# A decoder layer with routed experts on one core: routing of the first tiles inside the loop, routing lots and the prologue laid out anew

## The chip, the core and the metric

The kernel runs on one core of a Trainium2 chip. The core has five engines with a queue each: TensorE (PE, with its weight loads shown as PEld) multiplies matrices into eight PSUM banks, VectorE (DVE), ScalarE (ACT) and GpSimd (POOL) work on SBUF and PSUM, and SyncE (SP) issues most of the DMAs. An engine runs its queue in order and waits on semaphores that other engines or DMAs raise. The metric is device time in microseconds, lower is better.

## What is computed

Eight tiles of 128 rows with 256 features go through self attention, cross attention and a feed-forward part with 16 routed experts and a shared one:

```python
x = x + attn(layernorm(x), Wq, bq, Wk, bk, Wv, bv, Wo, bo)       # 16 heads, 4 key groups, rope, sliding mask
x = x + xattn(layernorm(x), ctx, ctx)                            # 16 heads, causal, keys = values = ctx
h = layernorm(x)
shared = silu_and_mul(h @ shared_gate_up_w.T) @ shared_down_w.T * sigmoid(h @ sgate_w.T)
w = softmax(h @ gate_w.T); top_w, top_ids = top_k(w, 4)
for e in range(16):
    coef = sum(where(top_ids == e, top_w, 0))
    acc += (silu_and_mul(h @ w13[e].T) @ w2[e].T) * coef
x = x + shared + acc
```

## The kernel before

Each engine's queue is written out by hand; no scheduler orders anything. A tile is one batch entry.

**Prologue.** GpSimd clears constants; TensorE runs bf16 matmuls on zeros (`keep_clock`, counts in `WARM`) between the first real steps. For tile f, `front_n` (VectorE) writes the first norm, `front_a` turns it on TensorE, `front_b` projects it to `qkv`, `front_r` (VectorE, L865) adds the bias, `turn` (GpSimd, L481 to L485) applies the rotation, `front_p` (VectorE, L870) pads the keys, and `front_c` turns queries and keys into the layout of the scores. `first_norms` makes the statistics of the input tiles, in lots of 2, 2 and 4 tiles.

**The loop.** Iteration t holds the self attention of tile t, the cross attention of tile t-1, the cross rows of tile t-2 (`cross_rows`, whose addition to x2 is L939) and the third norm of tile t-3, with the fronts of tiles t+1 and t+2. Iterations three to five are a hardware loop, the others are written out. In iteration t GpSimd also splits a chunk of the shared expert's weights into a high part (L517) and a low part (L519, the difference): an fp32 product is made as three matmuls of high and low parts (`three`, L1459).

**Routing.** For a lot of tiles: `logits` (24 matmuls for four tiles), `route_shift` and `route_exps` (softmax numerators), `route_top` (the four largest and their experts), `route_pick` (a mask of the picks), `ranks` (matmuls that count earlier rows of the same expert) and `route_slots` (L1007 to L1011), which writes for each row and pick a row number in a DRAM buffer, `x_slots`. Lots are tiles 0 to 3, 4 to 6, and 7. All of it stands behind the loop, in PSUM bank 2.

**Behind the loop.** The last cross attention, eight chunks of the first half of the shared expert (`rows_of`, `gate`, `gated`, `high_hidden`, `low_hidden`, `down`) and the split of the experts' weights: ScalarE copies the high parts of 16 experts (L746), VectorE makes the low parts of 13 (`low_expert`, L1165), GpSimd those of the last three (L597). GpSimd scatters the rows: per tile and pick one indirect DMA of 128 rows into `x_slots` (L531), 32 in all. Its queue also holds the deviation of each norm (`inverse_deviation`, L503) and a copy of each tile's third norm (`keep_rows`, L526).

**Expert blocks.** When all scatters have landed, SyncE loads 47 blocks of 128 rows from `x_slots` (`load_rows`), each is turned (L1692), multiplied by its expert's weights and scattered to `y_picks` (L604). Then the second half of the shared expert, the sums and the stores.

GpSimd's queue behind the loop, before:

```python
inverse_deviation(CROSS, B - 2)
pool.wait_ge(xn3_kept, LOT); pool.wait_ge(slots_ready, 1)
scatter(0, 0, 2); keep_rows(B - 2); scatter(0, 2, 4); scatter(1, 0, 2)
inverse_deviation(CROSS, B - 1)
scatter(1, 2, 3); keep_rows(B - 1); scatter(1, 3, 4); scatter(2); scatter(3)
pool.wait_ge(slots_ready, 2); scatter(4); scatter(5); scatter(6)
pool.wait_ge(slots_ready, 3); scatter(7)
```

## Time and profile before

| what | value |
|---|---|
| time, median of 3 runs | 369.44 us (368.15 to 370.2) |
| profiled execution: time, span | 368.4 us, 366.6 us |
| TensorE busy | 310.2 us (85%) |
| VectorE busy | 249.1 us (68%) |
| ScalarE busy | 187.7 us (51%) |
| GpSimd busy | 146.9 us (40%) |
| mean granted TensorE clock | 0.952 |
| chain that ended last, by engine | issue 26%, PE 25%, POOL 20%, DVE 18% |
| chain, by line: y_picks L604, x_slots L531 | 12%, 7% |

Busy time is an average over stages with different limits. The stages, by the timeline: prologue to about 23 us, the loop's iterations to about 144, the stretch behind the loop to about 217, the expert blocks to about 336, the end. A row of a timeline gives start and duration in us, engine, line, operation, output and input, and in square brackets how long the engine had been idle and who released it. The granted clock is the share of TensorE's full 2.4 GHz; its lower level is 1.2 GHz.

### The profile page before, as it was taken

The numbers are of one execution on the slowest core, as the hardware profiler recorded it, in microseconds if no ns is written. First come the engines' busy times: TensorE is split into PE (matmuls) and PEld (weight loads), VectorE is DVE, ScalarE is ACT, GpSimd is POOL, SyncE is SP. The second block draws the span as 40 slices with busy tenths as digits, with TensorE's granted clock in tenths as the row PEclk, the third lists the DMA queues.
The fourth block names the chain that finished last, engine by engine and source line by source line (L and its number), as shares of the span: only waits on it lengthen the run. The fifth ranks groups of instructions, "written<-read, shape, count | busy, mean of one in ns | idle before, by whom it ended". The sixth has DMA issues, their size and how long they took to land.

```text
span 366.6 us, 8490 instructions
## 1 busy us (share of the span) xinstructions
PE 310.2 (85%) x2595; PEld 239.8 (65%) x2596; DVE 249.1 (68%) x733; ACT 187.7 (51%) x537; POOL 146.9 (40%) x179
## 2 busy tenths in 40 slices
PE   6867799999989797877999239999899998999954
PEld 1434566767657566665777129888788987988743
DVE  1354789989998878777686406666567765763686
ACT  1025689888898967287674104334344443441210
POOL 2345323546344322144687762344344334444000
PEclk9898999999999899989999858999999999999995
DMA  5995089989979801001123432776777777773941
GB/s 206 295 386 240 4 247 242 299 238 248 305 211 303 228 12 31 0 32 61 47 106 122 174 91 90 224 212 204 215 203 227 230 217 209 226 234 108 361 154 57
DMA packets 44186, 66.84 MB, mean 182 GB/s; under 512 B 5380, under 2 KB 32021, under 8 KB 43637
## 3 DMA queue, kind: packets, MB, share of 16 engines
q1 hardware_dynamic: 39508, 54.91, 51.4%
q0 software_dynamic: 3792, 10.56, 7.7%
q10 hardware_dynamic: 848, 0.92, 0.8%
q8 instruction: 19, 0.31, 0.4%
q14 instruction: 19, 0.15, 0.1%
HBM read 37.07 MB, written 29.30 MB: 181 GB/s over the span
## 4 chain that ended last, share of the span: by engine, by line
issue 26%; PE 25%; POOL 20%; DVE 18%; DMA 5%; ACT 4%; DVEq 0%; SPq 0%; POOLq 0%; ACTq 0%
POOL y_picks L604 12%; POOL x_slots L531 7%; PE bank L1385 5%; PE bank L1332 3%; PE bank L1376 3%; PE bank L1459 3%; PE bank L1394 2%; DVE neg_max L882 2%; DMA rope<-rope_in_dram 2%; ACT probs L641 2%; PE bank L1497 2%; PE bank L1433 2%; PE bank L1418 1%; DVE x L939 1%; DVE yg L1282 1%
## 5 line engine op out<-in xcount | busy, mean ns | idle before, releaser
L604 POOL DMA_INDIRECT y_picks<-yb,ids x47 | 45.1, 959 | 75.2 <-DVE yb L1249 74.6
L641 ACT ACTIVATE probs<-bank,neg_max 128x128 f32<-128x128 f32 x256 | 70.9, 394 | 7.5 <-DVE neg_max L882 7.5
L1722 PE MATMUL bank<-w,hbt 128*128 128x256 f32 x188 | 48.2, 380 | 0.0
L882 DVE TENSOR_REDUCE neg_max<-bank 128x4 f32<-128x512 f32 x64 | 42.0, 681 | 5.0 <-PE bank L1376 5.0
L798 ACT ACTIVATE xbt_h<-bank 128x256 fp32r<-128x256 f32 x47 | 18.1, 384 | 49.1 <-PE bank L1692 49.0
L1385 PE MATMUL bank<-ident,probs 128*128 128x128 f32 x256 | 38.9, 292 | 3.8 <-ACT probs L641 3.8
L531 POOL DMA_INDIRECT x_slots<-x,slots x32 | 33.8, 1057 | 13.6 <-issue 9.1
L1385 PEld LDWEIGHTS bank<-ident,probs 128*128 128x128 f32 x256 | 31.1, 150 | 11.7 <-ACT probs L641 9.6
L1234 DVE TENSOR_TENSOR xbt_l<-bank,xbt_h 128x256 fp32r<-128x256 f32 x47 | 19.9, 424 | 22.4 <-ACT xbt_h L798 19.1
L1722 PEld LDWEIGHTS bank<-w,hbt 128*128 128x128 f32 x188 | 32.1, 190 | 2.5
L1692 PE MATMUL bank<-ident,xb 128*128 128x128 f32 x94 | 19.4, 290 | 16.5 <-DMA xb<-x_slots 16.3
L1242 DVE TENSOR_TENSOR hb<-sg,bank 128x176 f32<-128x176 f32 x47 | 15.9, 337 | 24.4 <-ACT sg L806 24.4
L806 ACT ACTIVATE sg<-bank 128x176 f32<-128x176 f32 x47 | 14.9, 318 | 30.5 <-PE bank L1459 30.5
L1692 PEld LDWEIGHTS bank<-ident,xb 128*128 128x128 f32 x94 | 12.3, 145 | 24.6 <-issue 13.3
L1459 PE MATMUL bank<-w_h,xbt_h 128*128 x94 | 27.7, 376 | 0.2 <-DVE xbt_l L1234 0.2
L481 POOL TENSOR_TENSOR turned<-qkv,rope 128x320 f32<-128x320 f32 x8 | 6.9, 864 | 49.6 <-DVE qkv L865 49.6
L503 POOL TENSOR_TENSOR rstd<-ve,expo 128x1 f32<-128x1 f32 x16 | 9.4, 590 | 39.7 <-DVE ve L932 39.7
L1249 DVE TENSOR_SCALAR yb<-bank,offset 128x256 f32<-128x256 f32 x47 | 22.7, 483 | 2.4 <-PE bank L1722 2.4
L1459 PE MATMUL bank<-w_l,xbt_h 128*128 x94 | 23.2, 329 | 0.0
L1459 PE MATMUL bank<-w_h,xbt_l 128*128 x94 | 23.1, 327 | 0.0
L813 ACT ACTIVATE hbt<-bank 128x256 f32<-128x256 f32 x47 | 18.1, 385 | 2.4 <-PE bank L1712 2.4
L1712 PE MATMUL bank<-ident,hb 128*128 128x128 f32 x94 | 18.1, 274 | 1.1 <-issue 0.9
(175 smaller groups left out, 683.2 us busy)
## 6 DMA issues: line engine op xcount, KB each, us to landing
x_slots<-zero_b SPq DMA_DIRECT2D x16, 1072.0 KB, 11.3
w<-w_in_dram SPq DMA_DIRECT2D x47, 256.0 KB, 3.1
xb<-x_slots SPq DMA_DIRECT2D x47, 134.0 KB, 2.9
w<-w_in_dram SPq DMA_DIRECT2D x4, 1408.0 KB, 12.9
yg<-y_picks SPq DMA_DIRECT2D x8, 512.0 KB, 7.2
sw_raw<-shared_in_dram SPq DMA_DIRECT2D x6, 384.0 KB, 3.5
ktc<-keys_in_dram SPq DMA_DIRECT2D x8, 256.0 KB, 2.8
ctx_sb<-ctx_in_dram SPq DMA_DIRECT2D x1, 1024.0 KB, 13.3
```

Source lines behind the costliest of these rows:

```text
L531: pool.indirect_dma_start(x_slots[:, :], bass.IndirectOffsetOnAxis(slots[:, TOPK * b + k:TOPK * b + k + 1], 0), x[:, b, :], None).then_inc ...
L604: pool.indirect_dma_start(y_picks[:, :], bass.IndirectOffsetOnAxis(ids[:, n:n + 1], 0), yb[:, n % RB, :], None).then_inc(yb_placed[n % RB] ...
L641: ins = act.activation(probs[:, g, j, :], ps_s[kind][g][:, 128 * j:128 * j + 128], ACT.Exp, bias=neg_max[:, kind, g, j:j + 1])
L798: act.activation(xbt_h[:, n % 2, :, :], ps_xt[n % 2][:, 0:KC * 128].rearrange("p (k n) -> p k n", k=KC), ACT.Copy).then_inc(xbt_high, 1)
L813: act.activation(hbt[:, n % 2, :, :], ps_ht[n % 2][:, 0:KC * 128].rearrange("p (k n) -> p k n", k=KC), ACT.Copy).then_inc(hbt_ready, 1)
L882: dve.tensor_reduce(neg_max[:, kind, g, :], ps_s[kind][g].rearrange("p (j n) -> p j n", j=BLK), AX.X, ALU.max, negate=True).then_inc(max_r ...
L1234: dve.tensor_tensor(xbt_l[:, n % 2, :, :], ps_xt[n % 2][:, 0:KC * 128].rearrange("p (k n) -> p k n", k=KC), xbt_h[:, n % 2, :, :].bitcast( ...
L1249: dve.tensor_scalar(yb[:, n % RB, :], ps_yb[n % 2][:, 0:D], offset[:, n % RB, 1:2], None, ALU.mult).then_inc(yb_ready, 1)
L1385: ins = pe.transpose(ps_s[kind][g][:, 128 * j:128 * j + 128], probs[:, g, j, :], ident[:, :])
L1459: ins = pe.matmul(outs, w, m, start=first and i == 0, stop=last and i == len(todo) - 1, skip_group_check=not (first and last))
L1692: ins = pe.transpose(ps_xt[n % 2][:, 128 * k:128 * k + 128], xb[:, n % RB, 128 * k:128 * k + 128], ident[:, :])
L1722: ins = pe.matmul(ps_yb[n % 2][:, 0:D], hbt[:, n % 2, k, :], w2[:, n % RB, k, :], start=k == 0, stop=k == KC - 1)
```

## The change

- **Prologue.** VectorE makes the first norm of tile 0 ahead of its wait for the rope table, and the statistics of tiles 4 to 7 inside iteration 0, behind the first two row maxima. TensorE turns and projects tile 1 before the 22 warming matmuls and the queries' turn of tile 0. Waits are added where tile 1 reuses `qkv` and `qk`.
- **The loop.** `split_shared(c)` on GpSimd waits for `x3_ready`, which the addition of the cross rows of tile c raises. Some waits of the fronts that others imply are dropped.
- **Routing of tiles 0 to 3.** `logits(0)` goes into iteration six, `route_shift(0)` and `route_exps(0)` between iterations six and seven, `route_top(0)` into iteration seven, pick, ranks and slots right behind. Routing moves from bank 2 to bank 7 (`ps_w`), which the turns use too, so waits keep these apart.
- **Lots** are tiles 0 to 3, 4 and 5, 6 and 7.
- **Behind the loop.** The first chunk of the shared expert is done in one piece, ahead of `ranks(0)`; high and low parts of the experts are spread out and stand later; banks 2, 3 and 4 change roles.

```diff
-        LOTS = (slice(0, LOT), slice(LOT, B - 1), slice(B - 1, B))
-        ps_r = [pb[2], pb[2], pb[2]]
+        LOTS = (slice(0, LOT), slice(LOT, B - 2), slice(B - 2, B))
+        ps_r = [ps_w, ps_w, ps_w]
...
             def split_shared(c):
                 pool.wait_ge(sw_loaded, 16 * c + 16)
+                pool.wait_ge(x3_ready, c + 1)
...
-            iteration(-2)
+            front_r(0)
+            front_n(1)
+            front_v(0)
+            front_r(1)
             dve.wait_ge(x_rest, 16)
             first_norms(LATER[0])
-            iteration(-1)
-            first_norms(LATER[1])
-            dve.wait_ge(rstd1_ready, 2)
+            front_p(0)
             iteration(0)
...
-            for t in (B - 2, B - 1):
-                iteration(t)
+            iteration(B - 2)
+            route_shift(0)
+            iteration(B - 1)
...
-            route_shift(0)
+            route_pick(0)
             add_rows(B - 1)
             statistics(SELF, B - 1)
-            route_top(0)
+            route_slots(0)
             second_norm(B - 1)
             third_norm(B - 3)
-            route_pick(0)
             cross_rows(B - 2)
...
             gated(0)
-            route_slots(1)
             cross_rows(B - 1)
             statistics(CROSS, B - 1)
+            route_slots(1)
             low_hidden(0)
+            low_expert(0)
             third_norm(B - 1)
...
             route_pick(2)
+            low_expert(3)
             gated(4)
-            for e in range(6, 11):
-                low_expert(e)
             route_slots(2)
             low_hidden(4)
+            low_expert(4)
             block_counts()
+            low_expert(5)
...
-            low_expert(11)
+            for e in range(6, 10):
+                low_expert(e)
             gated(SC)
             finish(0)
             low_hidden(SC)
+            low_expert(10)
+            low_expert(11)
             low_expert(12)
...
             project(B - 1)
             cross_values(B - 2)
             pe.wait_ge(probs_t_ready[SELF][2], B)
-            rows_of(0, [0])
+            pe.wait_ge(probs_t_ready[SELF][3], B)
+            rows_of(0)
+            pe.wait_ge(x2_ready, B)
+            ranks(0)
+            turn_values(CROSS, B - 2)
+            pe.wait_ge(slots_ready, 1)
             cross_queries(B - 1)
```

TensorE's queue at the start, before; `zero_b` are the warming matmuls, `xn` the norm of tiles 0 and 1, `xt` its turned copy, `qk` and `k_pad` queries and keys of tile 0:

```order
L1497 MATMUL bank<-zero_b 128x512 x13
L1323 MATMUL bank<-ident,xn_120 128x128 x2
L1497 MATMUL bank<-zero_b 128x512 x3
L1332 MATMUL bank<-wqkv,xt_121 128x384 x2
L1497 MATMUL bank<-zero_b 128x512 x22
L1341 MATMUL bank<-ident,qk 128x128 x2
L1345 MATMUL bank<-ident,k_pad 128x128 x2
L1323 MATMUL bank<-ident,xn_120 128x128 x2
L1332 MATMUL bank<-wqkv,xt_121 128x384 x2
```

The same place of TensorE's queue now:

```order
L1530 MATMUL bank<-zero_b 128x512 x13
L1346 MATMUL bank<-ident,xn_120 128x128 x2
L1530 MATMUL bank<-zero_b 128x512 x3
L1362 MATMUL bank<-wqkv,xt_121 128x384 x2
L1346 MATMUL bank<-ident,xn_120 128x128 x2
L1362 MATMUL bank<-wqkv,xt_121 128x384 x2
L1530 MATMUL bank<-zero_b 128x512 x22
L1373 MATMUL bank<-ident,qk 128x128 x2
L1377 MATMUL bank<-ident,k_pad 128x128 x2
```

The turn and the projection of tile 1 moved ahead of the 22 warming matmuls.

GpSimd's queue behind the loop, before; `rstd` is a deviation, `x<-xn` the copy of a third norm, `x_slots` the scatters, `w_l` the low parts:

```order
L503 TENSOR_TENSOR rstd_72<-ve_71,expo 128x1
L531 DMA x_slots<-x,slots 16512x268 x2
L526 COPY x<-xn_81 128x256
L531 DMA x_slots<-x,slots 16512x268 x4
L503 TENSOR_TENSOR rstd_72<-ve_71,expo 128x1
L531 DMA x_slots<-x,slots 16512x268
L526 COPY x<-xn_81 128x256
L531 DMA x_slots<-x,slots 16512x268 x25
L597 TENSOR_TENSOR w_l<-w_112,w_h 128x704 x3
```

The same place of GpSimd's queue now:

```order
L534 DMA x_slots<-x,slots 16512x268
L505 TENSOR_TENSOR rstd_72<-ve_71,expo 128x1
L534 DMA x_slots<-x,slots 16512x268 x3
L529 COPY x<-xn_81 128x256
L534 DMA x_slots<-x,slots 16512x268 x10
L505 TENSOR_TENSOR rstd_72<-ve_71,expo 128x1
L534 DMA x_slots<-x,slots 16512x268
L529 COPY x<-xn_81 128x256
L534 DMA x_slots<-x,slots 16512x268 x17
L600 TENSOR_TENSOR w_l<-w_112,w_h 128x704 x3
```

The last tile's deviation stood behind six scatters and now stands behind fourteen.

## Rows read from the trace of the kernel before

**Rows 1.** TensorE timeline at the first expert block: start us, us, instruction, [idle before <-releaser]
```profile
216.79 0.66 PE L1692 MATMUL bank<-ident,xb 128*128 128x128 f32 x2 [13.10 <-DMA xb<-x_slots]
```

**Rows 2.** Chain that ended last, scatters to first expert matmul: start us, us, what
```profile
179.05 1.34 POOL x_slots L531
...
210.69 2.47 DMA x_slots<-x,slots
...
218.55 2.14 PE bank L1459 x6
```

**Rows 3.** GpSimd timeline, scatters and the splits behind them
```profile
160.79 1.21 POOL L531 DMA_INDIRECT x_slots<-x,slots  x1 [4.58 <-DVE slots L1011]
...
167.32 1.52 POOL L531 DMA_INDIRECT x_slots<-x,slots  x1 [0.30 <-issue]
...
176.16 0.94 POOL L503 TENSOR_TENSOR rstd<-ve,expo 128x1 f32<-128x1 f32 x1 [5.72 <-DVE ve L932]
...
211.67 4.91 POOL L597 TENSOR_TENSOR w_l<-w,w_h 128x704 fp32r<-128x704 f32 x3
```

**Rows 4.** Chain that ended last, prologue
```profile
1.75 7.81 DMA rope<-rope_in_dram
...
14.24 4.75 PE bank L1497 x22
...
21.09 1.57 PE bank L1332 x4
...
23.31 1.31 DVE stat L849 x4
...
26.98 0.67 DVE k_pad L870
```

**Rows 5.** GpSimd timeline, first deviations
```profile
5.50 0.73 POOL L471 TENSOR_TENSOR rstd<-ve,expo 128x2 f32<-128x2 f32 x1 [3.78 <-DVE ve L854]
```

**Rows 6.** DMA issues: out<-in engine op xcount, KB each, us to landing
```profile
wqkv<-wqkv_in_dram SPq DMA_DIRECT2D x1, 384.0 KB, 6.8
```

**Rows 7.** VectorE timeline, cross rows of iterations three, four, seven
```profile
74.03 0.43 DVE L939 TENSOR_TENSOR x<-attn_c,x 128x256 f32 x1
...
89.24 2.00 DVE L939 TENSOR_TENSOR x<-attn_c,x 128x256 f32 x1
...
137.56 1.90 DVE L939 TENSOR_TENSOR x<-attn_c,x 128x256 f32<-128x256 f32 x1
```

**Rows 8.** GpSimd timeline, weight split of iteration four
```profile
89.14 1.82 POOL L519 TENSOR_TENSOR sw_l<-sw_raw,sw_h 128x768 f32 x1 [0.17 <-POOL sw_h L517]
```

**Rows 9.** TensorE timeline, self scores of iterations three, four, six
```profile
66.05 1.17 PE L1376 MATMUL bank<-qkt 32*128 32x128 f32 x32
...
81.26 1.17 PE L1376 MATMUL bank<-qkt 32*128 32x128 f32 x32
...
113.00 1.17 PE L1376 MATMUL bank<-qkt 32*128 32x128 f32 x32
```

**Rows 10.** TensorE timeline, self values of iteration six
```profile
124.91 1.07 PE L1394 MATMUL bank<-probs_ts,v_pad 128*32 128x512 f32 x8 [2.32 <-DVE probs_ts L888]
```

**Rows 11.** TensorE timeline behind the loop
```profile
147.14 0.44 PE L1426 MATMUL bank<-ident,attn 128*128 128x128 f32 x2
...
151.15 0.62 PE L1459 MATMUL bank<-xth,sw_l 128*128 128x512 f32 x2
```

**Rows 12.** VectorE timeline, last tile's norm to the shared rows
```profile
177.14 0.41 DVE L944 TENSOR_SCALAR xn<-x,mv,rstd 128x256 f32<-128x256 f32 x1 [0.47 <-POOL rstd L503]
...
191.96 0.17 DVE L1011 SCALAR_TENSOR_TENSOR slots<-top_f,slot_s 128x4 uint32<-128x4 f32 x1
...
203.51 1.65 DVE L1158 SCALAR_TENSOR_TENSOR x<-bank,sig,x 128x256 f32<-128x256 f32 x4
```

**Rows 13.** One line of the kernel, L1165: durations in ns, min/median/max
```profile
L1165 DVE TENSOR_TENSOR w_l<-w,w_h x13: 816/884/1084, 163.0 to 201.8; 128x704 fp32r<-128x704 f32 x13
```

**Rows 14.** Busy us of each engine in one stretch, behind the last slots
```profile
192.10:205.20 13.10, 10.73 (x52) 8.02 (x50) 9.84 (x28) 5.13 (x9) 10.05 (x11) 1.00 0.50 170
```

More of the change, by code:

```diff
@@ L590, in _ @@
             scatter(5)
-            scatter(6)
             pool.wait_ge(xn3_kept, B)
             pool.wait_ge(slots_ready, 3)
+            scatter(6)
             scatter(7)
@@ L715, in iteration @@
                     take_probs_t(CROSS, t - 1, 2)
-            for t in range(-2, 3):
+            front_a(0)
+            front_a(1)
+            front_c(0)
+            for t in range(3):
                 iteration(t)
@@ L1026, in iteration @@
                     row_max(SELF, t, 1)
+                if isinstance(t, int) and t == 0:
+                    first_norms(LATER[1])
+                    dve.wait_ge(rstd1_ready, 2)
+                if isinstance(t, int) and t == B - 1:
+                    route_top(0)
                 if on(t, t + 2):
@@ L1095, in _ @@
                 iteration(t)
-            for t in (B - 2, B - 1):
-                iteration(t)
+            iteration(B - 2)
+            route_shift(0)
+            iteration(B - 1)
             def block_counts():
@@ L1182, in _ @@
             row_max(CROSS, B - 1, 3)
-            route_slots(0)
+            route_shift(1)
             take_probs_t(CROSS, B - 1, 1)
             take_xtl(B - 2)
-            low_expert(0)
-            low_expert(1)
-            route_shift(1)
-            for e in range(2, 6):
-                low_expert(e)
             route_top(1)
@@ L1339, in front_c @@
                 pe.wait_ge(qk_ready, f + 1)
+                if isinstance(f, int) and f == 0:
+                    pe.wait_ge(qkv_ready, 2)
                 for u in range(2):
@@ L1501, in iteration @@
                     scores(SELF, t)
+                if isinstance(t, int) and t == B - 1:
+                    pe.wait_ge(exps_ready, 2)
                 if on(t, t - 1):
@@ L1529, in iteration @@
                     transpose_probs(SELF, t, 3)
+                if isinstance(t, int) and t == B - 2:
+                    logits(0)
                 if on(t, t + 2):
@@ L1594, in _ @@
                 iteration(t)
-            for t in (B - 2, B - 1):
-                iteration(t)
+            iteration(B - 2)
+            iteration(B - 1)
             def down(n):
```

102 lines of the change are left out of this document (60 added, 42 removed).

## The prediction

> **What bounds the kernel now.** I read the 40 slices of the page first: TensorE is nearly full in the attention loop and in the expert blocks, and nearly empty in a hole between them. The timeline gives that hole its size: TensorE sat idle for 13.10 us before it turned the first block's rows [rows 1]. The chain of waits says what filled it: from 179.05 on it is one indirect scatter of GpSimd after another, the last begins at 210.69, and the first expert matmul follows 7.86 us later, at 218.55 [rows 2]. GpSimd's own timeline shows why the scatters are late: the first waited for VectorE's slot numbers until 160.79, and after six the queue stood for 5.72 us at the deviation of the last tile, until 176.16 [rows 3]. From 179.05 to 210.69 lie 24 steps, 1.32 us each. Behind the scatters GpSimd still makes the low parts of three experts, 4.91 us. The expert blocks and the end behind them are not touched in what they do; I let them move as one piece, so the question is when the first expert matmul starts.
>
> Three places ahead of it change: the prologue, the loop's iterations from the fourth on, and the stretch behind the loop. The profiled execution took 368.4 us with a span of 366.6; the sum is made against it. The median of the three runs, 369.44, lies 1.0 above it.
>
> **1. Prologue: -2.2 us.** Before, VectorE waits for the rope table, which lands at 9.56 [rows 4], ahead of the first norm, though the norm needs only the deviation, done at 6.23 [rows 5]. Now the norm comes first (6.3 to 6.7), its transposes go behind the 13 warming matmuls, and the first projection waits only for its weights, issued at 1.24 and landed 6.8 later [rows 6], so 8.1 to 9.7. The query add follows at 9.8 in place of 14.28, the second tile's norm (0.7), transposes (0.4), copy (0.4) and projection (1.57, [rows 4]) end at 13.5. There the 22 warming matmuls now stand: 4.75 us [rows 4], to 18.2; they hide the rotation on GpSimd and the key padding. The first tile's turn, its copy and its scores end at 21.0, where they ended at 24.9. Of these 3.9 us not all is kept: the statistics of tiles 4 to 7, which VectorE did from 23.31 while the scores ran, now stand behind the first two row maxima, and the padded keys of tile 1, on which TensorE waits, come behind them. The VectorE work between, maxima 1.28, statistics 1.92, norm 0.55, padding 0.67, is 4.4: 25.4 in place of 27.65 [rows 4]. That is -2.2. Bounds: -3.9 if the padding were not waited for, and -0.5 if GpSimd's bias additions slow VectorE there.
>
> **2. The weight split behind the cross rows: -1.3 us in iterations four and five.** The addition of the cross rows took 0.43 us in iteration three and 2.00 in four; in four it ended with GpSimd's subtraction, 89.14 to 90.96 [rows 7, 8]. The change makes GpSimd wait for the addition. Iteration three is the same experiment by chance, and it says what the time saved is worth: it lasted 15.21 us, while four and five together lasted 31.74 [rows 9], 0.66 more each. The rest of the 1.57 is lost to TensorE, which is late next. Queued behind the split are only the rotation of the tile after next, which starts some 6 us later, and on SyncE the next load of raw weights and the zeroing, needed an iteration later; I cost both at nothing. Should the split stall another instruction of VectorE instead, the term is 0; with the full 1.57 twice it is -3.1.
>
> The Trainium skill, "SBUF — State Buffer", section "Who interferes with whom", says that a VectorE instruction with two SBUF inputs and a GpSimd instruction that reads SBUF exclude each other for the whole instruction. Rows 7 and 8 agree, 2.00 beside 0.43. The same rule speaks against the change further down: VectorE's last three low parts now meet GpSimd's three; by it alone the sum ends about 3 us later than without it.
>
> **3. Behind the loop: -9.7 us.** For this part I use before's clock, from which the 3.5 us of parts 1 and 2 come off afterwards. Iterations six and seven: TensorE idled 2.32 us before the self values of six [rows 10]; the 24 gate matmuls, 2.7 us, now stand in that gap and push the self values by about 0.5. The maxima, exponentials and top-four of tiles 0 to 3 go into iteration seven, 1.4 us on VectorE, of which 0.7 replaces a wait. Against that the addition of seven loses 1.5 of its 1.90 [rows 7]. Net I take -1.3 at the last attention rows. Their turn needs no gate matmuls ahead of it any more: 143.9 in place of 147.14 [rows 11].
>
> Slots of tiles 0 to 3: from that turn to the end of the first shared half took 4.63 us [rows 11]; the second half (1.4), the ranks (0.3) and the four slot steps (1.25) bring 151.5. VectorE and the cross queries of the last tile wait for this, about 2.7 us, which cancels the lead: the last tile's cross attention starts where it did. GpSimd first keeps a row tile, so the first scatter starts at 153.8 in place of 160.79.
>
> Then the queue of GpSimd: one scatter 1.2, a deviation 0.6, three scatters, a copy 0.5, ten scatters, at 1.32 each: 173.3, and only then the last deviation (0.94 before, [rows 3]). So the last tile's third norm runs at 174.4 in place of 177.14 [rows 12]; VectorE, TensorE and ScalarE wait for it some 3 us. This is the new wait. From that norm to the last slots it was 15.0 us [rows 12]; the stretch loses two of five low parts (0.88 each, [rows 13]), and gains a second tile and more table loading: 14.7, so 189.1. GpSimd has by then done the two scatters, the copy and the eight of tiles 4 and 5 (188.1), so the last eight start at 189.3, the last of them 7 x 1.32 later, at 198.5 to 199.4. With the 7.86 us of rows 2 the first expert matmul could start at 206.4 to 207.3.
>
> Other conditions for that matmul: from the last slots to the end of the shared rows VectorE took 13.0 us, 192.13 to 205.16 [rows 12], with two low parts in it; now there are nine, 6.2 us more, of which the 3.3 that it idled there (9.84 busy of 13.10, [rows 14]) take half. So about 16.0, to 205.1, and 1.2 more to the first block's low rows: 206.4. GpSimd's three low parts, 1.64 each [rows 3], run at 199.5 to 204.4, beside VectorE's last three. As in rows 7 each may hold up the other: up to 3.3 us. First expert matmul: 206.4 at best, 210 at worst; the nearest row for the fight is a stall to the end, so I take 208.8. Against 218.55 that is -9.7.
>
> **Sum.** 368.4 - 2.2 - 1.3 - 9.7 = 355.2; on the median's scale 356.2. I predict 356.
>
> **Rivals.**
> A, the weights become the end. High and low parts were pushed back into the last 15 us. If ScalarE's high parts or the fight cost 5 to 7 us more, part 3 gives 3 to 5 and the kernel takes 361 to 363. For it: the seven low parts moved there; against: VectorE had 3.3 us idle there.
> B, the prologue's clock. After 13.10 us of idling, two transposes took 0.66 [rows 1] against 0.44 for two behind busy matmuls [rows 11]. If small gaps around the second projection leave the array at its lower level (1.2 GHz), the 22 warming matmuls cost up to 9.5: 4.7 later, 361. Against: the array idles less ahead of them than before.
> C, the routing gains nothing. If ranks and slots, now tied into the last bank's turn order, hold the cross attention of the last tile back as long as the scatters win, only parts 1 and 2 remain: 366.
> D, slower. The scatters themselves stretch: the one at 167.32 took 1.52, a step of 1.82, beside VectorE's low parts [rows 3]. Those now lie spread along all scatters. Fourteen scatters stand ahead of the last deviation and eight behind the last slots, 22 on the path: at 1.82 the gain falls to 2 us; from 2.0 each the change loses, and at 2.1 it gives 356.2 + 22 x 0.78 = 373. Against: only a few of before's scatters were long, and the mean of 1.32 has them in it.
> E, better: no fight, no loss from the statistics, and the low clock at the start of the blocks avoided: 351.
>
> **How the numbers follow.** Forecast (352 to 360) 0.68, A 0.12, B 0.05, C 0.05, D 0.05, E 0.05. The range 351 to 363 holds the forecast, E, A and B. About 0.5% is what a measurement of this kernel can tell from no change, 1.8 us. All but D and a worse C are faster by more: 0.91; within 0.5% 0.04; slower 0.05.
>
> **What would show it.** In the profile after: padded keys of tile 1 near 25.4; every cross-rows addition near 0.43 and iterations of 15.2; first scatter near 150 (153.8 less 3.5); a wait of VectorE's third norm for GpSimd near 171; the last scatter near 195; first expert matmul near 205. The forecast is wrong if the iterations stay at 15.9, if a scatter takes longer than 1.4 in the mean, or if the matmul waits for low parts and not for rows.

## The result, and the profile after

The changed kernel takes 360.31 us (median of four executions, 359.31 to 360.82) where the kernel before takes 369.82 (four, 368.15 to 372.82). The ratio is 0.9731, 95% interval 0.9664 to 0.9798: 2.7% faster. The forecast was 356, range 351 to 363. The profiled execution took 359.31 us with a span of 357.5, 9.1 us under that of before; the sum had 13.2.

Nearly every mark of the forecast is late, by 3 to 7 us from the last attention rows on ("forecast" has the 3.5 us of parts 1 and 2 taken off):

| mark, us | before | forecast | after |
|---|---|---|---|
| padded keys of tile 1 turned | 27.69 | 25.4 | 25.18 |
| self scores of tile 1 | 37.45 | 35.2 | 36.76 |
| self scores of tile 7 | 129.82 | - | 129.98 |
| last attention rows turned | 147.14 | 140.4 | 144.96 |
| slots of lot 0 | 159.65 | 148 | 152.22 |
| first scatter | 160.79 | 150.3 | 154.08 |
| third norm of tile 7 | 177.14 | 171 | 173.85 |
| last slots | 191.96 | 185.6 | 188.68 |
| last scatter starts | 210.69 | 195 | 202.23 |
| first expert matmul | 218.55 | 205 | 210.43 |
| from there to the end | 148.05 | 148.05 | 147.07 |

TensorE's timeline in the prologue shows the forecast turn of the keys (beside [rows 4]), and tile 1's scores hardly earlier:

```profile
25.18 0.69 PE L1377 MATMUL bank<-ident,k_pad 128*128 128x128 f32 x2 [4.04 <-DVE k_pad L881]
...
36.76 1.17 PE L1409 MATMUL bank<-qkt 32*128 32x128 f32 x32
```

What lies between, and later, is seen in four stretches (from:to, length, busy us of PE, PEld, DVE, ACT and POOL with their instructions, granted clock, DMA share, GB/s):

```profile
24.00:36.00 12.00, 8.98 (x35) 5.56 (x36) 4.71 (x10) 4.13 (x12) 1.87 (x3) 0.59 0.70 295
122.00:130.00 8.00, 8.00 (x58) 5.74 (x58) 3.57 (x11) 3.84 (x14) 0.00 (x0) 0.57 0.60 187
146.00:172.00 26.00, 21.54 (x204) 16.72 (x205) 14.69 (x57) 13.20 (x33) 15.95 (x20) 0.87 0.18 64
204.00:222.00 18.00, 12.92 (x65) 11.44 (x66) 12.11 (x33) 5.01 (x15) 6.42 (x5) 0.72 0.33 93
```

The column before the last two is the one to read. Before, the same stretches had 0.86, 0.79, 0.93 and 0.62. TensorE runs at 2.4 or at 1.2 GHz; 0.59 over 12 us is some 10 us at the lower. It is there from 24, near the end of the 4.04 us wait for the keys, until 34, and of 2.5 us lead 0.7 are left. In iteration six the narrow gate matmuls come first:

```profile
120.68 0.36 PE L1492 MATMUL bank<-gate_h,xth 128*128 128x18 f32 x2 [0.15 <-DVE xtl L970]
...
123.53 0.57 PE L1492 MATMUL bank<-gate_h,xtl 128*128 128x18 f32 x2
124.04 1.94 PE L1427 MATMUL bank<-probs_ts,v_pad 128*32 128x512 f32 x8
...
129.98 1.17 PE L1409 MATMUL bank<-qkt 32*128 32x128 f32 x32
```

A pair of them goes from 0.36 to 0.57 us as the clock falls at about 122.7, and the self values behind take 1.94 where they took 1.07 [rows 10]. At 110.94 the scores of tile 6 were 2.06 us ahead of before, at 129.98 those of tile 7 are 0.16 behind. VectorE's timeline behind the loop (the answer to [rows 12]):

```profile
152.22 0.17 DVE L1024 SCALAR_TENSOR_TENSOR slots<-top_f,slot_s 128x16 uint32<-128x16 f32 x1
...
169.56 0.26 DVE L916 RECIPROCAL inv_c<-bank 128x16 f32<-128x16 f32 x1 [3.67 <-PE bank L1451]
...
173.85 0.41 DVE L957 TENSOR_SCALAR xn<-x,mv,rstd 128x256 f32<-128x256 f32 x1
...
188.68 0.17 DVE L1024 SCALAR_TENSOR_TENSOR slots<-top_f,slot_s 128x8 uint32<-128x8 f32 x1
```

The forecast wait of the third norm for GpSimd is not there: its row has no brackets. VectorE had waited 3.67 us for TensorE instead, whose clock was low from 160 to 167. At the end, GpSimd (beside [rows 3]), then VectorE, then TensorE (beside [rows 1]):

```profile
195.31 3.84 POOL L534 DMA_INDIRECT x_slots<-x,slots  x1 [0.30 <-issue]
...
202.23 1.30 POOL L534 DMA_INDIRECT x_slots<-x,slots  x1 [0.30 <-issue]
203.56 4.92 POOL L600 TENSOR_TENSOR w_l<-w,w_h 128x704 fp32r<-128x704 f32 x3
```

```profile
195.09 3.22 DVE L1186 TENSOR_TENSOR w_l<-w,w_h 128x704 fp32r<-128x704 f32 x4
...
204.79 4.25 DVE L1165 TENSOR_TENSOR hid_l<-hid,hid_h 128x512 fp32r<-128x512 f32 x1
```

```profile
208.68 0.66 PE L1732 MATMUL bank<-ident,xb 128*128 128x128 f32 x2 [7.38 <-POOL w_l L600]
...
210.43 0.95 PE L1492 MATMUL bank<-w_h,xbt_h 128*128 x2
```

One scatter took 3.84 us (195.31 to 199.15) while VectorE made four low parts back to back (195.09 to 198.31), and the last eight went at 1.80 a step instead of 1.32. The first block waited for GpSimd's low parts until 208.48, though its rows were in at about 208.1 (issued 206.0, median 2.1 us to land). GpSimd's low parts took 4.92 us beside VectorE, as long as before (4.91), so the fight did not lengthen this wait. TensorE's 13.10 us hole is 7.38.

So three suspects: TensorE's low level, the meeting of scatters and low parts, and a tie that was costed from two iterations. The experiments take them in turn. "After" in a reading of a trace below is the profiled execution above. The medians below are over all executions of a kernel, while the ratios leave out those over 1.5% slower than its fastest.

### The profile page after: what moved, and what is told of

It is laid out like the page before. It is cut to its first block, busy times and chain, and to the rows that moved or that the text cites. A ratio compares the mean times of both kernels' runs of the same rounds, so it can differ in the third digit from the quotient of the medians.

```text
span 357.5 us, 8484 instructions
## 1 busy us (share of the span) xinstructions
PE 312.9 (88%) x2594; PEld 242.3 (68%) x2595; DVE 247.5 (69%) x733; ACT 186.6 (52%) x537; POOL 149.0 (42%) x179
## 4 chain that ended last, share of the span: by engine, by line
PE 35%; issue 23%; POOL 16%; DVE 13%; ACT 6%; DMA 4%; SPq 0%; POOLq 0%; DVEq 0%; ACTq 0%
POOL y_picks L607 12%; PE bank L1492 7%; PE bank L1418 6%; PE bank L1409 5%; PE bank L1362 4%; POOL x_slots L534 3%; PE bank L1427 3%; ACT probs L644 2%; PE bank L1451 2%; PE bank L1404 2%; PE bank L1530 2%; PE bank L1466 2%; DVE yg L1304 1%; DVE neg_max L895 1%; DMA yg<-y_picks 1%
## 5 line engine op out<-in xcount | busy, mean ns | idle before, releaser
L1418 PE MATMUL bank<-ident,probs 128*128 128x128 f32 x256 | 39.8, 297 | 3.0 <-ACT probs L644 3.0
L534 POOL DMA_INDIRECT x_slots<-x,slots x32 | 36.7, 1147 | 10.8 <-issue 8.9
L743 ACT ACTIVATE hid_h<-hid 128x512 fp32r<-128x512 f32 x12 | 7.6, 632 | 28.3 <-DVE hid L1160 28.3
L505 POOL TENSOR_TENSOR rstd<-ve,expo 128x1 f32<-128x1 f32 x16 | 9.4, 590 | 28.5 <-DVE ve L945 28.4
```

Of the source, the lines that this page charges most:

```text
L534: pool.indirect_dma_start(x_slots[:, :], bass.IndirectOffsetOnAxis(slots[:, TOPK * b + k:TOPK * b + k + 1], 0), x[:, b, :], None).then_inc ...
L1418: ins = pe.transpose(ps_s[kind][g][:, 128 * j:128 * j + 128], probs[:, g, j, :], ident[:, :])
```

## Experiments

Two kernels measured in different sessions are compared by their ratios; the difference of two ratios is uncertain by some 3 to 4 us.

| kernel | median, us | ratio to before, 95% interval |
|---|---|---|
| changed kernel | 360.31 | 0.9731 (0.9664 to 0.9798) |
| before, with the tie | 364.43 | 0.9856 (0.9770 to 0.9943) |
| after, without the tie | 365.36 | 0.9881 (0.9787 to 0.9976) |
| after, lot 0 behind the loop | 361.22 | 0.9799 (0.9715 to 0.9882) |
| after, wide matmuls in iteration six | 360.19 | 0.9753 (0.9688 to 0.9819) |
| after, warming behind the loop | 356.36 | 0.9651 (0.9560 to 0.9743) |
| after, warming at both ends | 354.77 | 0.9606 (0.9532 to 0.9681) |
| after, four low parts late | 360.21 | 0.9739 (0.9645 to 0.9832) |
| after, low parts early | 356.44 | 0.9639 (0.9558 to 0.9720) |
| after, warming in four places | 353.56 | 0.9561 (0.9510 to 0.9612) |
| before, warming in its waits | 367.05 | 0.9938 (0.9902 to 0.9974) |
| after, warming and low parts early | 350.53 | 0.9495 (0.9443 to 0.9548) |
| the last, without the tie | 355.39 | 0.9624 (0.9563 to 0.9686) |

### The tie alone, and the change without it

```diff
 pool.wait_ge(sw_loaded, 16 * c + 16)
+pool.wait_ge(x3_ready, c + 1)
 pool.tensor_copy(sw_h..., sw_raw...)
```

> The kernel before with one wait added: each half split of the shared weights follows the cross rows of its tile, as in the change; nothing else. Theory (the cross-row add loses up to 1.6 us beside the split, in the iterations where they meet): the add at 0.43 us in all eight, scores of tile 7 at 128.2 to 128.6 instead of 129.82, the kernel 1.0 to 2.0 us under before. Rival 1 (the split's later end holds back the next piece of shared weights or the padded keys): within 0.5 us of before. Rival 2 (an iteration that comes out 1.5 us earlier changes where TensorE's low clock falls behind the loop, and that is worth more than the add): 3 us or more under before, most of it behind 145.

Measured: 4.4 us under before in the medians (2 to 8.5 us by the interval of the ratio), more than either of the first two texts. The line of the addition in the kernel before and in the one with the tie (durations in ns: min/median/max), the addition of iteration six before with the split beside it, and the scores of tiles 6 and 7 with the tie:

```profile
L939 DVE TENSOR_TENSOR x<-attn_c,x x8: 424/1392/2003, 59.3 to 174.8; 128x256 f32<-128x256 f32 x5, 128x256 f32 x3
```

```profile
L940 DVE TENSOR_TENSOR x<-attn_c,x x8: 424/425/426, 61.3 to 173.3; 128x256 f32<-128x256 f32 x5, 128x256 f32 x3
```

```profile
120.74 1.90 DVE L939 TENSOR_TENSOR x<-attn_c,x 128x256 f32<-128x256 f32 x1
...
120.54 1.81 POOL L519 TENSOR_TENSOR sw_l<-sw_raw,sw_h 128x768 fp32r<-128x768 f32 x1
```

```profile
113.66 1.17 PE L1377 MATMUL bank<-qkt 32*128 32x128 f32 x32
...
128.02 1.17 PE L1377 MATMUL bank<-qkt 32*128 32x128 f32 x32
```

The gain lies inside the loop, not behind 145 as the second rival had it: from the scores of tile 1 to those of tile 7 88.53 us in place of 92.37, 0.7 in each of iterations four and five as forecast, and 2.5 in iteration six, where the addition was shorter and before's clock had fallen while here it did not (before first, then with the tie):

```profile
122.00:130.00 8.00, 5.68 (x51) 3.87 (x53) 6.80 (x17) 6.24 (x20) 0.41 (x2) 0.79 0.77 221
```

```profile
122.00:130.00 8.00, 6.65 (x91) 4.76 (x89) 7.05 (x18) 6.81 (x23) 3.15 (x3) 1.00 0.81 237
```

From the scores of tile 7 to the last attention rows, iteration seven, it is another 1.1. The prologue, whose queues are the same, was 2.0 us slower here (tile 1's scores at 39.49 for 37.45), so the whole span is only 3.0 us shorter. The opposite, the tie taken from the changed kernel:

```diff
 pool.wait_ge(sw_loaded, 16 * c + 16)
-pool.wait_ge(x3_ready, c + 1)
```

> The changed kernel without the wait that ties each half split of the shared weights to the cross rows; all else as changed. Theory (the tie takes the 1.6 us that the cross-row add loses beside the split in the iterations where they meet): the add takes up to 2.0 us again in some of tiles 0 to 5 instead of 0.43, the loop is 1 to 2 us longer, and the whole kernel 361.3 to 362.3 us against 360.3. Rival 1 (waits later in the loop and low clock behind it swallow it): 360.0 to 360.6. Rival 2 (the tie holds GpSimd's other work back, a mean 1.8 us wait per iteration, and costs more than it saves): below 360.0.

Measured: 365.36, 5 us slower; all three texts miss. The trace shows two parts: the scores of tile 7 come 0.8 later and the last attention rows 1.9, and from there to the third norm it takes 3.5 us longer, at a clock of 0.70 where after had 0.87:

```profile
146.00:172.00 26.00, 21.40 (x186) 16.55 (x185) 14.30 (x56) 14.13 (x37) 14.89 (x18) 0.70 0.16 59
```

The low level alone does not explain the medians: the mean clocks of the four executions are 0.936 to 0.940, those of after 0.934 to 0.944.

### Routing of lot 0 put back behind the loop

```diff
 iteration(B - 2)
-route_shift(0)
 iteration(B - 1)
+route_shift(0)
+route_top(0)
```

The same move is made for `logits(0)` and the wait for its exponentials on TensorE, and for `route_exps(0)` on ScalarE.

> The changed kernel with the first steps of lot 0's routing (gate matmuls, shift, exponentials, top four) taken out of iterations six and seven and put behind the loop, ahead of the turn of the last tile's attention, in the new order otherwise. Theory of the forecast (routing inside the loop fills waits and brings the first slots 9 us forward): the slots of lot 0 come 3 to 5 us later than 152.2 and the kernel is 3 or more us slower, 363 to 365. Rival (the 24 narrow matmuls in iteration six cost the 2 us lead that they were to use, so in the loop is worth little): scores of tile 7 at 127.8 instead of 129.98, attention of tile 7 turned at 144 to 145 as now, and the kernel within 1.2 us of 360.3.

Measured: 361.22, 0.9 us over after in the medians and 2.5 by the ratios, whose intervals overlap: no difference that these runs can tell, though one of several us isn't excluded. The time is the rival's; its mark of 144 to 145 is not. Without the narrow matmuls iteration six takes 14.3 us instead of 19.0, and the attention rows are turned at 141.02, 3.9 us ahead of after (1.6 of it from the prologue, where nothing was changed). All of it is gone at the third norm:

```profile
149.63 0.17 DVE L1024 SCALAR_TENSOR_TENSOR slots<-top_f,slot_s 128x16 uint32<-128x16 f32 x1
...
174.69 0.40 DVE L957 TENSOR_SCALAR xn<-x,mv,rstd 128x256 f32<-128x256 f32 x1
```

```profile
146.00:172.00 26.00, 21.97 (x164) 17.44 (x163) 12.18 (x44) 12.32 (x32) 15.57 (x19) 0.67 0.20 75
```

What an earlier lot 0 gains is paid back between the attention rows and the third norm, which the next runs look into.

### TensorE kept busy in its waits

All use the same kind of matmul, whose result nobody reads:

```diff
+def warm(bank, n):
+    for _ in range(n):
+        pe.matmul(bank[:, :], zero_b[:, 0:128], zero_b[:, 0:HALF], start=True, stop=True)
```

First only in iteration six:

```diff
 for b in range(bs.start, bs.stop):
     ins = three(... gate_h ... gate_l ...)
+    if i == 0:
+        warm(ps_o, 2)
```

> The changed kernel with eight warming matmuls (128x512 of zeros, 0.21 us each, 1.7 us in all, into the bank that the values of tile 6 overwrite next) among the 24 narrow gate matmuls of iteration six, two behind each tile's six. Theory (the narrow matmuls end with a TensorE at its low level, and the 1.94 us of the self values, 1.97 us of the transposes and twice 1.06 us behind them should be 1.07, 1.05, 0.6 and 0.65): granted clock 1.0 in 122 to 130, 2.6 us back for 1.7 us spent, scores of tile 7 at 129.1 instead of 129.98, and the kernel 359.0 to 360.0 us. Rival (the clock falls for another reason, or something else than TensorE sets iteration seven): the clock stays at 0.5 to 0.7 there and the scores come 1.7 us later, 361 to 362 us.

Measured: 360.19. The clock held and the scores of tile 7 came at 128.52, 1.5 us earlier; but behind the loop the clock was low for longer and the third norm came at 174.26, 0.4 later. The time did not follow the mark:

```profile
122.00:130.00 8.00, 7.70 (x98) 5.51 (x96) 4.46 (x15) 4.35 (x16) 0.68 (x2) 1.00 0.74 213
146.00:172.00 26.00, 21.97 (x188) 17.45 (x179) 13.15 (x54) 12.74 (x32) 16.07 (x19) 0.74 0.20 74
```

Nor is the earlier mark all the edit's. The same iteration without the eight, which lasted 19.0 us in after, lasted 17.5, 17.4 and 15.9 in three later traces (four low parts late, warming at both ends, warming behind the loop), and 17.4 with them. They hold the clock, but they stand in TensorE's own time and cost 1.5 us where it would have held anyway.

Then behind the loop:

```diff
+warm(pb[3], 5)
 pe.wait_ge(slots_ready, 1)
 cross_queries(B - 1)
+warm(pb[3], 2)
 scores(CROSS, B - 1)
 third_norm(B - 3)
+pe.wait_ge(x3_ready, B - 1)
+warm(ps_o, 7)
 transpose_probs(CROSS, B - 1, 0)
+warm(ps_o, 1)
 transpose_probs(CROSS, B - 1, 1)
```

and `warm(ps_o, 2)` behind the gate matmuls of each tile of lot 1.

> The changed kernel with warming matmuls (128x512 of zeros, 0.21 us each) in TensorE's waits behind the loop: five ahead of the wait for the first slots, two ahead of the cross scores of tile 7, seven and one ahead of the transposes of its weights, four among the gate matmuls of lot 1. Theory (the time that an earlier lot 0 gains is given back because TensorE waits at 151 to 158, falls to its low level and does the values, the shared rows and the transposes of 160 to 167 at it): the granted clock stays at 1.0 from 150 to 170, VectorE's 3.67 us wait for the cross values of tile 7 shrinks to under 2 us, the third norm of tile 7 comes 2 to 3 us before 173.85 (or then waits for GpSimd's deviation), and the kernel is 357.5 to 359 us. Rival (GpSimd's fourteen scatters ahead of the last deviation set the third norm anyway): the clock stays up, the norm moves under 1 us, 359.8 to 361 us.

Measured: 356.36 in the median, 4 us under after (3.0 by the ratios, whose intervals overlap). The marks of the theory are met: the clock is 1.00, VectorE's wait for the cross values 1.97 us, and the wait of the forecast appears where VectorE is no longer late, 1.45 us for GpSimd's deviation.

```profile
146.00:172.00 26.00, 22.95 (x197) 16.29 (x196) 15.72 (x56) 12.72 (x33) 17.87 (x21) 1.00 0.21 75
```

```profile
170.22 0.41 DVE L957 TENSOR_SCALAR xn<-x,mv,rstd 128x256 f32<-128x256 f32 x1 [1.45 <-POOL rstd L505]
```

Not all of its 3.6 us at the third norm is the edit's: in this execution the clock also held through iteration six, where nothing was changed, which gave 3.1. In the stretch that was edited this trace is 0.4 us shorter than after's. What the edit itself does is seen over all traces of the changed kernel's versions, from the turn of the last attention rows to the third norm of tile 7, against the clock in 146 to 172:

| kernel | from, to, us | length | clock |
|---|---|---|---|
| lot 0 behind the loop | 141.02, 174.69 | 33.7 | 0.67 |
| without the tie | 146.84, 179.21 | 32.4 | 0.70 |
| wide in iteration six | 143.50, 174.26 | 30.8 | 0.74 |
| warming at both ends | 140.59, 171.11 | 30.5 | 0.80 |
| four low parts late | 141.59, 172.12 | 30.5 | 0.80 |
| after | 144.96, 173.85 | 28.9 | 0.87 |
| low parts early | 145.19, 174.05 | 28.9 | 0.87 |
| warming behind the loop | 141.70, 170.22 | 28.5 | 1.00 |
| warming in four places | 142.70, 171.18 | 28.5 | 1.00 |
| warming and low parts early | 139.77, 168.27 | 28.5 | 1.00 |
| the last, without the tie | 143.20, 171.68 | 28.5 | 1.00 |

The four with warming there are the last four rows: always 1.00 and 28.5 us. The five whose TensorE queue is after's in this stretch (wide in iteration six, both ends, four low parts late, after, low parts early) take 28.9 to 30.8, so the edit is worth 0.4 to 2.3 us here; the rest of the 4 us in the medians isn't shown to be its work.

Third, the two ends, ahead of the wait for tile 1's padded keys and behind the turn of the shared rows:

```diff
+if isinstance(f, int) and f == 1:
+    warm(pb[3], 17)
 pe.wait_ge(k_padded, f + 1)
...
+warm(pb[4], 30)
 pe.wait_ge(hid_ready, SC + AHEAD)
```

> The changed kernel with warming matmuls in two other waits of TensorE: 17 in the 4.04 us wait for the padded keys of tile 1 in the prologue, and 30 behind the turn of the shared rows at 201.3, in the 7.38 us wait ahead of the first expert block. Theory (the low level that follows each wait is what the prologue's 2.5 us lead was lost to, and what the first blocks pay): scores of tile 1 at 34.8 to 35.1 instead of 36.76 with a granted clock of 1.0 in 25 to 34, and 1 to 2 us less from the first expert matmul to the end than 147.07 us; the kernel 357 to 358.8 us. Rival (warming keeps the clock, but the prologue's lead is lost again in the loop and the blocks are held by their transfers): 359.8 to 361 us.

Measured: 354.77, better than expected. Scores of tile 1 at 33.94, 2.8 us earlier, and 145.84 us from the first expert matmul to the end, 1.2 less than after:

```profile
24.00:36.00 12.00, 8.60 (x92) 4.97 (x90) 7.21 (x16) 4.37 (x14) 4.18 (x7) 1.00 0.69 294
...
204.00:222.00 18.00, 16.52 (x96) 13.56 (x95) 12.31 (x39) 6.90 (x21) 5.62 (x6) 1.00 0.52 143
```

Only the earlier scores can be put down to the edit, and in part: without it tile 1's scores came at 34.92 to 36.92 in seven traces, with it at 33.92 to 34.01 in three and at 36.08 in a fourth, whose clock fell behind 30. The 1.2 us are within the scatter of that stretch, which takes 144.2 to 148.5 us over all versions of the changed kernel, 144.2 to 147.0 in the four whose blocks start at the upper level. And 1.6 us of this trace's lead come in iteration six, where nothing was changed.

### Scatters beside low parts

```diff
-for e in range(6, 10):
-    low_expert(e)
 gated(SC)
 ...
-low_expert(10)
-low_expert(11)
-low_expert(12)
 gated(SC + 1)
 ...
 low_hidden(SC + 1)
+for e in range(6, 13):
+    low_expert(e)
```

Experts 10 to 12 move as well; in after they stood beside the last two scatters, not beside the long one.

> The changed kernel with VectorE's four back-to-back low parts of experts 6 to 9 (195.09 to 198.31) moved behind the last shared hidden piece, so that they no longer stand beside the last eight scatters. Theory A (the scatter that took 3.84 us was held by them): no scatter over 1.5 us, a step of 1.25 to 1.35 us instead of 1.80, the last scatter starts at 198.5 to 199.3 instead of 202.23; the rows could then be in at 204.5 to 205.5, but seven low parts of VectorE and three of GpSimd stand at the end together, 207 to 210, so the first expert matmul comes within 1.5 us of 210.4 and the kernel is 359.5 to 362 us: the work is moved, not removed. Theory B (the scatters' own transfers are slow there): the step stays 1.7 to 1.9 us and the low parts come on top, 362 to 364 us.

Measured: 360.21. Theory A: no scatter over 1.45 us and a step of 1.35 (187.88 to 197.36); the fifth of the eight, which took 3.84 in after, is this one. GpSimd was done at 203.28, but VectorE's seven low parts now end last:

```profile
193.56 0.96 POOL L534 DMA_INDIRECT x_slots<-x,slots  x1 [0.30 <-issue]
```

```profile
203.76 5.69 DVE L1186 TENSOR_TENSOR w_l<-w,w_h 128x704 fp32r<-128x704 f32 x7
```

```profile
209.55 1.09 PE L1729 MATMUL bank<-ident,xb 128*128 128x128 f32 x4 [9.98 <-DVE w_l L1186]
```

The work was moved, not removed. To remove it from the end it has to go where VectorE waits:

```diff
 gated(1)
+low_expert(1)
 low_hidden(1)
 take_xtl(B - 1)
-low_expert(1)
+low_expert(2)
 gated(2)
+low_expert(3)
 low_hidden(2)
-low_expert(2)
+low_expert(4)
...
-for e in range(6, 10):
-    low_expert(e)
+low_expert(10)
```

On ScalarE, `high_experts(2, 6)` stands ahead of `high_hidden(1)`, and the later groups follow two to four earlier.

> The changed kernel with ScalarE's high parts of the expert weights issued as early as the cross rows of tile 7 allow (four at 171 instead of two at 176) and VectorE's low parts one at a time in its waits of 0.7 to 0.9 us from 174 to 184, so that only experts 10 to 12 are left behind 193, none of them back to back. Theory (the end of the routing is set by the volume of low parts that VectorE and GpSimd do beside and behind the last eight scatters, 13 of VectorE's 16 x 0.81 us piling up behind 185): the last eight scatters go at 1.25 to 1.4 us a step, the last starts at 198 to 200, the first expert matmul comes at 206 to 208 instead of 210.43, and the kernel is 356.5 to 358.5 us. Rival (the low parts put into the waits push the slots of lot 2 back by as much): slots 2 us later than 188.68, first expert matmul at 210 or later, 360 to 361.5 us.

Measured: 356.44, the theory's time, 3.9 us under after in the median (3.4 by the ratios, whose intervals overlap). Two executions with a mean clock of 0.94, like after's, took 357.79 and 358.29, some 2 us under after; two at 0.957 and 0.956 took 355.09 and 354.60, so part of the median is the clock. The slots of lot 2 came at 188.89, not later, and the longest of the last eight scatters took 1.60 us (a step of 1.42). But the profiled execution (358.29, the slowest of its four) started its first expert matmul at 209.73, not at 206 to 208, because one low part of VectorE met GpSimd's three:

```profile
201.34 5.74 DVE L1187 TENSOR_TENSOR w_l<-w,w_h 128x704 fp32r<-128x704 f32 x1
```

A low part that takes 0.81 us undisturbed took 5.74: the fight of the forecast, on another instruction.

### What is left when the clock is held

The four insertions together in the changed kernel (lot 0 and lot 1 with two wide matmuls per tile), and the like in the kernel before, whose edit is:

```diff
+    warm(pb[3], 5)
 pe.wait_ge(qk_ready, f + 1)
...
+    warm(pb[3], 4)
 pe.wait_ge(k_padded, f + 1)
...
+    pe.wait_ge(x3_ready, B - 3)
+    warm(ps_o, 10)
 self_values(t)
...
+pe.wait_ge(x3_ready, B - 1)
+warm(ps_o, 9)
 transpose_probs(CROSS, B - 1, 0)
...
+warm(pb[4], 56)
 pe.wait_ge(hid_ready, SC + AHEAD)
```

> The changed kernel with warming matmuls (128x512 of zeros) in all four places where TensorE waits and then runs at its low level: 17 in the prologue, eight among the gate matmuls of iteration six (1.7 us of TensorE's own time), fifteen behind the loop, 30 ahead of the first expert block. With the next kernel it asks what the change itself is worth when neither kernel loses time to the low level. Theory (my sum of 13.2 us was right as the work is laid out, and the shortfall to 9.1 is the low level): this kernel at 351 to 353 us and the kernel before with the same treatment 11 to 13.5 us above it. Rival (the gain of 9 us was itself largely the low level, since the tie alone brought 4.4 us instead of 1.3): 351 to 353 us, and before only 6 to 9 us above it.

> The kernel before with warming matmuls in its waits: nine in the prologue beside the padded keys of tile 1, ten in the 2.32 us wait of iteration six, nine in the 2.06 us wait behind the loop, 56 in the 13.10 us ahead of the first expert block. From rows of before: low level in 27 to 32, 126 to 130, 156 to 161 and 208 to 222 us; about 1.0, 1.8, 1.5 and 1 to 2 us come back, 363 to 365 us against 368.9. Theory of the last kernel's text: 11 to 13.5 us above that kernel; rival: 6 to 9.

Measured: 353.56 and 367.05, 13.5 us apart. The number falls into the theory's 11 to 13.5, but the comparison is not clean, and it isn't taken as proof of the sum. The changed kernel held its clock behind the prologue, not in it; before regained 2 us where 4 to 6 were expected, for its clock then fell at other places (the changed kernel's row first, then before's, of the same stretches):

```profile
24.00:36.00 12.00, 9.06 (x59) 4.23 (x57) 5.76 (x14) 4.08 (x13) 2.60 (x4) 0.86 0.65 273
...
146.00:172.00 26.00, 22.96 (x197) 16.27 (x196) 15.51 (x56) 12.41 (x32) 17.52 (x21) 1.00 0.21 75
```

```profile
24.00:36.00 12.00, 9.48 (x50) 4.59 (x43) 5.88 (x13) 6.09 (x20) 7.85 (x12) 0.86 0.58 243
...
146.00:172.00 26.00, 23.19 (x215) 17.41 (x215) 17.49 (x63) 14.48 (x37) 10.86 (x12) 0.87 0.07 27
```

What it does show is the changed kernel's path with TensorE at its upper level: third norm 171.18 with a wait of 1.46 for GpSimd (forecast 171), last slots 185.67 (185.6), last scatter 199.22 (195), first expert matmul 207.19 (205).

Everything that helped, together, with GpSimd's three low parts given to VectorE:

```diff
-for e in range(13, NE):
-    pool.wait_ge(w13_high, e + 1)
-    pool.tensor_tensor(w13_l[:, e, :, :], w13[:, e, :, :], ...)
...
 gated(SC + 1)
-low_expert(12)
+for e in range(12, NE):
+    low_expert(e)
```

> All that helped, together: the changed kernel with warming matmuls in the four places (four instead of eight in iteration six, 28 ahead of the first block), ScalarE's high and VectorE's low parts early and one at a time as in the run before, and GpSimd's last three low parts given to VectorE. Expected from the parts: 3.6 us (behind the loop, as its own trace shows it), 2.8 (prologue), 1.2 (first blocks), 2 to 4 (low parts) under 360.3, less what overlaps: 348 to 351 us, the last scatter 197 or earlier and the first expert matmul 6 to 8 us behind it, set by the rows' landing. If the low parts only move the wait (rival): 352 to 354.

Measured: 350.53, in the expected range, and the fastest kernel of this study, 5.0% under before. The last scatter starts at 193.75, the first expert matmul at 202.82, 9.1 behind it where 6 to 8 were expected, and each of the four stretches has a clock of 1.00. It was not set by the rows' landing, as expected: the block's turn at 201.35 stands right behind the 28 warming matmuls (195.30 to 201.51), while VectorE's low parts were done at 198.58 and its rows, issued at 197.85, were in at about 200 (2.1 us to land, as in after). So many warming matmuls cost up to 1.4 us here, an estimate from these rows. This kernel is the place to ask again what the tie is worth:

```diff
-pool.wait_ge(x3_ready, c + 1)
```

> The last version (warming in four places, low parts early) without the wait that ties the half splits to the cross rows. The tie was worth 4.4 us alone on the kernel before and 5.0 us in the changed kernel, where the forecast had 1.3 (two iterations of 0.66). Theory (the add itself is worth 0.7 us in each iteration where it meets the split, some 2 us in all, and the rest was TensorE's low level, which lasts longer when the loop comes out later): with the clock held, the loop up to the scores of tile 7 is 1.3 to 2.2 us longer than in that version, what lies behind it is not, and the kernel is 351.8 to 353 us against 350.5. Rival (the tie is worth its 4 to 5 us whatever the clock, for instance because the shared weights arrive in a better order): 354.5 to 356 us.

Measured: 355.39 against 350.53, 4.8 us by the two ratios (uncertain by 3), so the rival's number, but not its reason. The clock held here too, and the trace shows the loss inside the loop. The line of the addition, the scores of tile 7 and the first expert matmul without the tie, and the last two with it:

```profile
L948 DVE TENSOR_TENSOR x<-attn_c,x x8: 424/1387/2002, 55.7 to 166.5; 128x256 f32<-128x256 f32 x5, 128x256 f32 x3
```

```profile
127.16 1.17 PE L1415 MATMUL bank<-qkt 32*128 32x128 f32 x32
...
206.30 0.59 PE L1498 MATMUL bank<-w_h,xbt_h 128*128 x2 [0.87 <-DVE xbt_l L1255]
```

```profile
124.80 1.17 PE L1416 MATMUL bank<-qkt 32*128 32x128 f32 x32
...
202.82 0.59 PE L1499 MATMUL bank<-w_h,xbt_h 128*128 x2 [0.78 <-DVE xbt_l L1256]
```

Iterations four to seven are longer by 0.75, 0.74, 0.98 and 1.07 us without the tie: 3.5 in all, and the first expert matmul is later by the same 3.5. The split meets the addition in four iterations, not two. The other 1.3 us of the medians aren't in this trace: its execution (352.37) was the fastest of its six, and made up 2.3 us in the expert blocks.

## Why the prediction was right, and where it was off

The sign and the range hold: 360.3 lies in 351 to 363, 4 us above the forecast. In the profiles the sum of parts, 13.2, was 4.1 too large: up to tile 1's scores 0.7 us were gained (forecast 2.2), from there to the scores of tile 6 1.4 (forecast 1.3), from there to the first expert matmul 6.1 (forecast 9.7), behind it 1.0 (forecast nothing). Two of the prediction's three signs of being wrong were seen, the last scatters at more than 1.4 us a step and a matmul that waited for low parts, so the number held partly by luck and by a range of 12 us.

**1. Prologue, -2.2.** The instruction that was forecast came where it was forecast, 25.18 for 25.4. The term failed at its next step, that this lead would reach the loop: 0.7 did in this pair of traces. TensorE's wait of 4.04 us went with 10 us at its low level. Rival B had the mechanism and the wrong place, during the 22 warming matmuls instead of behind them. How much arrives is a matter of luck: with these queues tile 1's scores came at 34.92 to 36.92, with the old ones at 37.45 and, before with the tie, at 39.49. With the wait filled and the clock held they came at 33.94, 3.5 ahead of before.

**2. The tie, -1.3.** Mis-sized. The two iterations gained what was forecast (0.7 each), but the tie as a whole was worth 4.4 us alone, 5.0 in the changed kernel, and with the clock held 4.8 in the medians and 3.5 in the traces, where four iterations account for all of it. What the rest is stays open. [rows 7] had a long addition in iteration seven too; I put it into another term's net and left out iteration six (1.90 at 120.74). Of what was measured singly, this one wait is the largest part of the 9 us.

**3. Behind the loop, -9.7.** The order of events was right, its lead was not. The step that failed is the net of iterations six and seven: the gate matmuls were costed at 0.5 us in TensorE's gap, and with the low level behind them iteration six took 19.0 us, 2.2 more than before. With the clock held it took 15.9, still 1.5 more than the 14.3 without them. From the scores of tile 6 to the last attention rows 0.1 us was gained where 3.2 were forecast. The net itself was also summed wrongly: 0.5 and 0.7 against 1.5 make -0.3, not -1.3. Put behind the loop the routing steps cost the same in the end, as far as these runs can tell (361.22 to 360.31), so the part that the change is named for brought nothing that these runs can tell. The new wait of the third norm for GpSimd exists (1.45 us, forecast 3), but only when TensorE isn't the later one.

**The last stretch.** From the third norm to the end of the last slots 15.0 us, forecast 14.7. Then the scatters: 1.80 us a step for 1.32, 3.4 us in all. This is rival D's mechanism in one place instead of everywhere, and its cause is shown by the run that took the four low parts away. The fight of the low parts at the end was forecast at up to 3.3 us; the hidden rows' low part lost 3.6 to it, but VectorE, done at 209.04, was then idle for 0.83, so the block did not wait for that. Rival A stands in it too, small: GpSimd's low parts, not the rows, were last, by 0.4 us. The Trainium skill, "SBUF — State Buffer", section "Who interferes with whom", says that a DMA which seems stalled by VectorE is one that GpSimd issues, starved of its port while it makes descriptors. The trace agrees, 3.84 us beside four low parts and 0.96 without. For a `tensor_tensor`, which a low part is, the same section infers that it does not do this; here the measurement decides.

**The end.** It was to move as one piece; it became 1.0 us shorter. Why stays open: over all traces it takes 144.2 to 148.5 us, and in its first 6 us the clock was no better than before (0.63 for 0.72).

Not tried alone: the lots of 4, 2, 2 tiles, and the old prologue in the new kernel. What they bring by themselves stays open; of 9 us, the tie and the prologue's 0.7 leave 3 to 5 to them, to the new order and to the lucky or unlucky fall of the clock.

## What to carry to other kernels

An engine's lead is worth what the next wait leaves of it: ask of every microsecond gained where TensorE then stands idle, and fill that wait with matmuls into a bank that nobody reads (here 1.8% in four places). They are free only as long as they end before the wait does: eight in TensorE's own time cost 1.5 us. And they don't always hold the clock: in one of four traces it fell in the prologue all the same. A stall that is found in one iteration is to be looked for in all of them before it is costed. Two-input VectorE work on SBUF belongs where GpSimd is not scattering, one instruction at a time, not in a row beside the queue that everything waits for.

## What the runs showed of the hardware

- The same program text kept or lost its clock from one execution to the next. In the prologue after had 0.59 in 24 to 36, and two kernels that differ from it only behind that stretch (four low parts late, lot 0 behind the loop) 0.86 each; tile 1's scores came at 36.76, 34.92 and 35.12. In iteration six after had 0.57 in 122 to 130, and the run with warming only behind the loop 1.00. A single profile is no measure of such a term. The Trainium skill, "TensorE: Matmul & The Clock Gate", section "Part 1: The HAM clock gate", says of the first rise of the clock that the moment varies from run to run; the runs show the same of falls later in a kernel. Warming in four places brought 1.8% by the ratios (medians 360.31 and 353.56).
- In after TensorE was busy for all 8.00 us of 122 to 130, most of it behind 24 narrow matmuls (128x18), and had a granted clock of 0.57; with eight wide ones among them it was busy for 7.70 and had 1.00. In the 12 us from the first gate matmul on, the four traces with wide ones had 1.00, the six without 0.72, 0.72, 0.86, 0.86, 0.86 and, once, 1.00. That a full row of busy time can hide the lower level I had not expected.
- An indirect scatter of 128 rows beside four back-to-back subtractions of VectorE took 3.84 us instead of 0.96; beside single ones 1.1 to 1.6. In the other direction a subtraction of 0.81 us took 5.74 beside three of GpSimd's.
